# A mixture-of-experts kernel whose sort by expert becomes lists in DRAM, filled chunk by chunk during conditioning

## The chip, the cores and the metric

One core of one Trainium2 chip. The metric is the device time of one execution in microseconds.

## What is computed

```python
def cond(x, W, A, Bm, scalings, adapter_idx):      # x: 64 x 64 x 512, f32
    delta = (x @ A[adapter_idx].T) @ Bm[adapter_idx].T * scalings[adapter_idx]
    return x @ W.T + delta                         # rank 16, 8 adapters
def ffn(x, ...):                                   # 4096 tokens of 512
    shared = sum(gelu(x @ Wsh_up[e]) @ Wsh_down[e] for e in range(2))
    top_v, top_i = top_k(softmax(x @ W_router), 2) # of 16 experts
    routed = sum(top_v[r] * gelu(x @ Wrt_up[top_i[r]]) @ Wrt_down[top_i[r]] for r in range(2))
    return shared + routed                         # hidden 256 per expert
out = x + ffn(cond(x))
```

## The kernel before, in words

4096 tokens are 16 chunks of 256 (`NC`), each two tiles of 128. Most fp32 products are done as three fp16 products: each matrix is scaled by a power of two taken from its largest magnitude, a high half is rounded to fp16 (ScalarE) and the low half is what is left (VectorE or GpSimd). Every engine runs its own written-out queue; semaphores order them.

**Conditioning.** For each chunk c TensorE's `cond_step` (L1278) does the adapter input (L1238), two tiles of x @ W (L1249) with the transposes of chunk c-1 (L1265) between, the router logits of c-1 (L1274) and the adapter output (L1257). VectorE's step is `search_step` (L971) for chunks up to 7 and `low_step` (L1026) from chunk 8: `mask_xa` (L875, the first of a step), `row_max`, `x_low` for chunk c+1, `x_largest` for chunk c+2 (L947), maxima of arriving expert weights (`lot_maxima`, L906) or the low halves of two experts (`low_routed`, L935), `x_scales` (L952) and `top` (L881: logits copied, the two best of 16 and their indices, L883 to L893). GpSimd spreads the maximum of x over the partitions by an all-reduce (`x_reduce`, L521). Chunks 0 and 1 are multiplied whole in fp32 (`whole=True`), from chunk 2 on in halves. SyncE's `cond_chunk` (L352) loads chunk c+3, stores rows and transposes of chunk c, and `weights_chunk` issues the next two expert loads, each after a wait on `lot_max_ready`; the load of the next x stands behind these.

**Sort.** After the last chunk VectorE makes one-hots of all tokens (L1051), TensorE their prefix sums (L1301), VectorE a scan over 32 tiles (L1063, L1064), the start of each expert's tiles (L1067 to L1081), the place of each token (L1083 to L1093) and the scales of the whole conditioned x, whose maximum comes back by way of DRAM (L404, L914). Then `places` (L1101) compares iotas with each place (L1107, L1108), 64 times two instructions, and `inversion_products` (L1310, matmul L1313) turn them on TensorE into `tok`, the token of each slot. `sorted_ready` lets GpSimd gather rows (`gather`, L566).

**Early shared passes.** Meanwhile TensorE does the shared experts of chunks 0 to 5 (`EARLY`): `shared_up` (L1327, 48 matmuls) and `shared_down` (L1340, 24), in an order written out by hand with the sort's products between. ScalarE rounds the high halves (L662, L767) and writes a scaled copy (L664, L769), from which GpSimd subtracts (`low_condT` L542, `low_hid` L547); GpSimd also does `add_x` (L537).

**Routed tiles.** 79 tiles of 128 slots, pipelined: transpose (L1377), up (L1393), transpose of the middle (L1402), down (L1412). GpSimd gathers the rows (L574).

**Late stage.** The shared passes of chunks 6 to 15, while GpSimd gathers routed rows back (L608) and VectorE adds them weighted (L1168).

What sets the order: an engine's instructions start in the order written, so what stands behind a wait waits as well. This is all that decides it on SyncE's and GpSimd's queues of DMAs too.

```python
with pe.Fori(1, A_HALF) as i:
    cond_step(2 * i, i, 0)
    cond_step(2 * i + 1, i, 1)
```

## Time and profile before

| what | us |
|---|---|
| median of 3 runs | 679.23 (679.11 to 682.99) |
| the profiled execution | 681.92 |
| its span, first to last instruction | 679.9 |
| mean granted TensorE clock | 0.974 |

The profile is one execution, so the sums are made against 681.92. Times in a timeline count from the start of the span. PE is TensorE, PEld its weight load, DVE VectorE, ACT ScalarE, POOL GpSimd, SP SyncE. "[3.63 <-DMA ...]" is the idle time of that engine just before the instruction and what ended it. The granted clock is in shares of full speed, 2.4 GHz. L is a line of the kernel.

### The profile page before, as it was taken

To read this page: it belongs to the slowest core of one execution; us is meant where nothing else is said; L and a number is where in the kernel's file an instruction comes from. 1 tells how busy PE (TensorE), PEld (TensorE's weight loads), DVE (VectorE), ACT (ScalarE), POOL (GpSimd) and SP (SyncE) were. 2 spreads that over 40 slices of the span, in tenths; PEclk is the share of its full clock that TensorE was granted. 3 is DMA by queue.
4 is the path that set the end of the run, shared out by engine and by line. 5 is a ranking of instruction groups with operands and counts; after the bars stand their busy time and mean duration, and the time that the engine had idled before them with its cause. 6 is when DMAs were issued, how large, how long until landed. Compare 5 with 4: busy or idle time off the path is not lost.

```text
span 679.9 us, 13742 instructions
## 1 busy us (share of the span) xinstructions
PE 627.5 (92%) x4115; PEld 428.4 (63%) x4117; DVE 457.4 (67%) x900; ACT 327.2 (48%) x480; POOL 222.6 (33%) x288
## 2 busy tenths in 40 slices
PE   4998999999989758889999999999999999989794
PEld 2465656566657435556777777777777777665561
DVE  2779999999974998525555555555555554688674
ACT  1333224677775743464555555555555554333230
POOL 1000000101012742373333333333333306777771
PEclk9997999999998988999999999999999999999898
DMA  7688994343334312165555555555555539989966
GB/s 275 281 312 286 374 346 168 123 157 142 132 127 128 124 63 93 32 217 171 159 159 169 161 154 159 164 168 157 156 159 167 164 107 377 366 301 362 369 205 248
DMA packets 49765, 135.68 MB, mean 200 GB/s; under 512 B 6160, under 2 KB 6288, under 8 KB 47312
## 3 DMA queue, kind: packets, MB, share of 16 engines
q1 hardware_dynamic: 38304, 97.93, 39.1%
q0 software_dynamic: 11440, 37.50, 20.0%
q8 instruction: 11, 0.18, 0.1%
q14 instruction: 10, 0.08, 0.0%
HBM read 86.38 MB, written 49.02 MB: 199 GB/s over the span
## 4 chain that ended last, share of the span: by engine, by line
PE 53%; DVE 17%; POOL 12%; issue 7%; DMA 7%; ACT 1%; SPq 0%; DVEq 0%; POOLq 0%; ACTq 0%
PE bank L1412 15%; PE bank L1393 14%; POOL rtw L608 9%; PE bank L1249 7%; PE bank L1377 5%; DVE lot_max L906 5%; DMA act_in<-xT 3%; PE bank L1402 2%; PE bank L1327 2%; PE bank L1257 2%; PE bank L1274 2%; DMA region<-xc_dram,slot_idx 2%; PE bank L1238 1%; DVE x_max L947 1%; PE bank L1265 1%
## 5 line engine op out<-in xcount | busy, mean ns | idle before, releaser
L1129 DVE SCALAR_TENSOR_TENSOR region<-bank,scale,region 128x512 f16<-128x512 f32 x79 | 59.2, 751 | 128.7 <-ACT region L809 128.7
L1393 PE MATMUL bank<-rtw,region 128*128 x948 | 116.4, 273 | 0.0
L1412 PE MATMUL bank<-rtw,tmp 128*128 x474 | 115.2, 379 | 0.6 <-DVE tmp L1137 0.6
L1393 PEld LDWEIGHTS bank<-rtw,region 128*128 128x128 f16 x948 | 92.8, 98 | 10.1
L1340 PE MATMUL bank<-shw,hid 128*128 128x512 f16 x384 | 91.3, 397 | 8.3 <-DVE rtw L1193 7.7
L574 POOL DMA_INDIRECT region<-xc_dram,slot_idx x79 | 77.1, 976 | 61.3 <-POOL slot_idx L571 61.3
L1327 PE MATMUL bank<-act_in,shw 128*128 128x256 f16 x768 | 89.4, 277 | 2.9 <-ACT tmp L756 1.7
L1327 PEld LDWEIGHTS bank<-act_in,shw 128*128 128x128 f16 x768 | 75.8, 100 | 16.0 <-ACT tmp L756 2.2
L816 ACT ACTIVATE region<-bank,un_dn 128x512 f32<-128x512 f32 x79 | 54.3, 687 | 57.3 <-PE bank L1412 54.8
L608 POOL DMA_INDIRECT rtw<-r_dram,row_idx x64 | 70.0, 1093 | 27.6 <-issue 14.8
L1340 PEld LDWEIGHTS bank<-shw,hid 128*128 128x128 f16 x384 | 38.4, 102 | 56.4 <-issue 10.0
L1412 PEld LDWEIGHTS bank<-rtw,tmp 128*128 128x128 f16 x474 | 46.3, 98 | 39.2 <-issue 1.3
L805 ACT ACTIVATE tmp<-bank,un_up 128x256 f32<-128x256 f32 x79 | 37.4, 473 | 60.2 <-PE bank L1393 60.2
L1168 DVE SCALAR_TENSOR_TENSOR rtw<-rtw,gate 128x512 f32 (+1 forms) x64 | 45.4, 750 | 15.2 <-DMA rtw<-r_dram,row_idx 13.0
L809 ACT ACTIVATE region<-bank,scale 128x512 f16<-128x512 f32 x79 | 54.1, 687 | 2.2 <-PE bank L1377 2.2
L523 POOL PARTITION_ALL_REDUCE x_max_all<-x_max x14 | 10.7, 763 | 134.9 <-DVE x_max L949 134.9
L1377 PE MATMUL bank<-ident,region 128*128 128x128 f32 x316 | 47.4, 273 | 2.6 <-DMA region<-xc_dram,slot_idx 2.5
L571 POOL COPY slot_idx<-tok 128x1 int32 (+1 forms) x79 | 14.4, 182 | 106.5 <-PE bank L1377 97.0
L756 ACT ACTIVATE tmp<-bank,un_up 128x256 f32<-128x256 f32 x44 | 20.4, 471 | 52.2 <-PE bank L1327 49.9
L641 ACT ACTIVATE rtw<-rtw,scale 128x1024 f16<-128x1024 f32 (+1 forms) x32 | 35.8, 1152 | 17.3 <-DVE rtw L935 15.1
L935 DVE SCALAR_TENSOR_TENSOR rtw<-rtw,scale 128x1024 f16<-128x1024 f32 x32 | 39.6, 1279 | 4.4 <-ACT rtw L641 4.3
L1135 DVE TENSOR_SCALAR tmp<-bank,to_mid 128x256 f16<-128x256 f32 x79 | 38.2, 484 | 6.1 <-PE bank L1402 2.7
(157 smaller groups left out, 910.0 us busy)
## 6 DMA issues: line engine op xcount, KB each, us to landing
r_dram<-region SPq DMA_DIRECT2D x79, 256.0 KB
rtw<-rt_w SPq DMA_DIRECT2D x16, 1024.0 KB, 7.4
act_in<-xT SPq DMA_DIRECT2D x16, 512.0 KB, 3.8
xc_dram<-rows SPq DMA_DIRECT2D x16, 512.0 KB, 3.7
xcT_dram<-hid SPq DMA_DIRECT2D x16, 512.0 KB, 2.8
rtw<-x_rows SPq DMA_DIRECT2D x16, 512.0 KB, 5.4
rtw<-xcT_dram SPq DMA_DIRECT2D x13, 512.0 KB, 6.1
out<-rtw SPq DMA_DIRECT2D x9, 512.0 KB, 5.6
```

The lines of the kernel that those rows point to most:

```text
L574: nc.gpsimd.indirect_dma_start(out=xg[s], out_offset=None, in_=xc_dram, in_offset=bass.IndirectOffsetOnAxis(ap=slot_idx[s][:].bitcast(U32) ...
L608: nc.gpsimd.indirect_dma_start(out=routed_row(slot, r, t), out_offset=None, in_=r_dram, in_offset=bass.IndirectOffsetOnAxis(ap=row_idx[slo ...
L809: nc.scalar.activation(xgT[s][:, 0], R_XT[s][:].rearrange("p (k t) -> p k t", k=HK), ACT.Copy, scale=col(scale, C_ALL).bitcast(F32)).then_ ...
L816: nc.scalar.activation(rrow[s], R_DN[s][:], ACT.Copy, scale=col(un_dn, ROUTED)).then_inc(rrow_ready, 1)
L1129: nc.vector.scalar_tensor_tensor(xgT[s][:, 1], R_XT[s][:].rearrange("p (k t) -> p k t", k=HK), col(scale, C_ALL).bitcast(F32), xgT[s][:, 0 ...
L1168: last = nc.vector.scalar_tensor_tensor(y, routed_row(slot, r, t), gate[:, r, bass.ds(c * NT + t, 1)], y, ALU.mult, ALU.add)
L1249: last = mm(COND[NT * s + t][:], act_in[s][:, k, at] if whole else xp[s][:, ap, k, at], w_in[:, k, :] if whole else wt[:, bp, k, :], start ...
L1327: last = mm(UP[em % 2][:, 0:CHUNK], shw[:, e, w0:w0 + P], actT[s][:, xp, k, :], start=(k == 0 and n == 0), stop=(k == HK - 1 and n == 2))
L1340: last = mm(DOWN[t][:], hidT[s][:, xp, em, t * P:(t + 1) * P], shw[:, em // DM, w0:w0 + H], start=(em == 0 and n == 0), stop=(em == EM - 1 ...
L1377: last = nc.tensor.transpose(R_XT[s][:, k * P:(k + 1) * P], xg[s][:, k * P:(k + 1) * P], ident[:])
L1393: last = mm(R_UP[s][:, 0:D], xgT[s][:, xp, k, :], rtw[:, bass.ds(e, 1), w0:w0 + D].rearrange("p a d -> p (a d)"), start=(k == 0 and n == 0 ...
L1412: last = mm(R_DN[s][:], midT[s][:, xp, m, :], rtw[:, bass.ds(e, 1), w0:w0 + H].rearrange("p a h -> p (a h)"), start=(m == 0 and n == 0), s ...
```

## The change

- **Lists.** A DRAM tensor `lists` has 4096 places for each expert. After `top` VectorE makes the chunk's one-hot; GpSimd's `count` adds them up and keeps the running count over earlier tiles; TensorE's `rank_products`, in the same turn as a later router product, give every token's rank; VectorE's `list_places` turns expert and rank into a place two steps later; GpSimd's `scatter` writes 128 token numbers by an indirect DMA, four a chunk. At the end VectorE works out from which 128-entry list each tile comes, GpSimd gathers these and TensorE transposes them into `tok`. The slot of each token for the way back (`pos`) is worked out after that.
- **Maxima.** The maximum per partition is put on a diagonal, TensorE multiplies it by ones (`spread_x`, `spread`) and VectorE reduces the row. The all-reduces and the way through DRAM are gone.
- **Chunk 1** is multiplied in halves; only chunk 0 whole. Its x comes into the place of expert 12's weights. The small loads are issued first and chunk 2's x before the shared weights.
- **Low halves** of the early shared passes are made by VectorE straight from the unscaled source; ScalarE's scaled copies are gone, GpSimd keeps `add_x`.
- `x_scales` stands after both `low_routed`, and the load of chunk 2's transpose is issued earlier.

The diff, cut to its core:

```diff
--- before
+++ after
+        lists = nc.dram_tensor("lists", [E_RT * LIST, P], F32, kind="Internal").ap()
...
-            sp.dma_start(at_in, AT).then_inc(w_adapters, 16)
-            sp.dma_start(flat(act_in[0][:]), chunk_T(xT, 0)).then_inc(act_loaded[0], 16)
             sp.dma_start(sc_col[:], scal).then_inc(w_mask, 16)
             sp.dma_start(idx_b[:], idx.partition_broadcast(P)).then_inc(w_mask, 16)
+            sp.dma_start(at_in, AT).then_inc(w_adapters, 16)
+            sp.dma_start(flat(x_first), chunk_T(xT, 0)).then_inc(first_loaded, 16)
             for dst, src in ((w_in, WT), (bmt, BmT), (wr, w_r)):
                 sp.dma_start(dst, src).then_inc(w_cond, 16)
-            sp.dma_start(flat(act_in[1][:]), chunk_T(xT, 1)).then_inc(act_loaded[1], 16)
+            for c in range(1, 3):
+                sp.dma_start(flat(act_in[c % 2][:]), chunk_T(xT, c)).then_inc(act_loaded[c % 2], 16)
+            sp.wait_ge(masks, 5)
+            sp.dma_start(lists.rearrange("(p a) n -> p (a n)", p=P), lg[:].rearrange("p t e -> p (t e)")).then_inc(lists_cleared, 16)
             sp.dma_start(arrived(0), sh_up).then_inc(w_shared, 16)
             sp.dma_start(spare, sh_dn).then_inc(w_shared, 16)
-            sp.wait_ge(act_used, 1)
-            sp.dma_start(flat(act_in[0][:]), chunk_T(xT, 2)).then_inc(act_loaded[0], 16)
...
+            sp.wait_ge(condT_half, 1)
+            load_condT(2, 0, early_condT(2))
...
-            def x_reduce(c, s):
-                pool.wait_ge(x_max_ready, c - 1)
-                nc.gpsimd.partition_all_reduce(x_max_all[s][:], x_max[s][:], P, RMAX).then_inc(x_reduced, 1)
...
+            def count(k, s):
+                at = slice(NT * k, NT * k + NT)
+                pool.wait_ge(top_ready, k + 1)
+                if k > 1:
+                    pool.wait_ge(rank_read, k - 1)
+                if k:
+                    nc.gpsimd.tensor_tensor(earlier[s][:, 0, :], earlier[1 - s][:, 1, :], oh_sum[1 - s][:, 1, :],
+                                            ALU.add)
+                nc.gpsimd.tensor_copy(best[:, at, :], best_c[s][:, :, 0:K_TOP])
+                nc.gpsimd.tensor_copy(chosen[:, :, at], best_i_c[s][:, :, 0:K_TOP].rearrange("p t r -> p r t"))
+                nc.gpsimd.tensor_tensor(oh_sum[s][:], oh[s][:, 0], oh[s][:, 1], ALU.add).then_inc(summed, 1)
+                pool.wait_ge(summed, k + 1)
+                nc.gpsimd.tensor_tensor(earlier[s][:, 1, :], earlier[s][:, 0, :], oh_sum[s][:, 0, :], ALU.add).then_inc(counted, 1)
+                pool.wait_ge(counted, k + 1)
+            def scatter(k):
+                pool.wait_ge(slot_ready, k + 1)
+                for r in range(K_TOP):
+                    for n in range(NT * k, NT * k + NT):
+                        nc.gpsimd.indirect_dma_start(
+                            out=lists.rearrange("a (n o) -> (a n) o", o=1),
+                            out_offset=bass.IndirectOffsetOnAxis(ap=pos[:, r, n:n + 1].bitcast(U32), axis=0),
+                            in_=tok_no[:, n:n + 1], in_offset=None,
+                        ).then_inc(scattered, 16)
+            pool.wait_ge(lists_cleared, 16)
+            for c in range(1, NC):
+                if c > 2:
+                    scatter(c - 3)
+                count(c - 1, (c - 1) % 2)
+            scatter(NC - 3)
+            count(NC - 1, 1)
+            scatter(NC - 2)
+            scatter(NC - 1)
+            pool.wait_ge(list_ready, 1)
+            pool.wait_ge(scattered, 16 * K_TOP * TT)
+            nc.gpsimd.indirect_dma_start(
+                out=tokT, out_offset=None, in_=lists,
+                in_offset=bass.IndirectOffsetOnAxis(ap=list_i[:].bitcast(U32), axis=0),
+            ).then_inc(tokT_loaded, 16)
...
-            low_condT(0)
-            low_condT(1)
-            for c in range(EARLY - 2):
-                low_hid(c)
-                low_condT(c + 2)
-                if c:
-                    add_x((c - 1) // 2, (c - 1) % 2)
-            low_hid(EARLY - 2)
+            for c in range(2):
+                add_x(0, c)
...
-                last = nc.scalar.activation(actT[s][:, 0], by_block(src), ACT.Copy, scale=by)
-                if early:
-                    last = nc.scalar.activation(src, src, ACT.Copy, scale=by)
-                last.then_inc(condT_half, 1)
+                nc.scalar.activation(actT[s][:, 0], by_block(src), ACT.Copy, scale=by).then_inc(condT_half, 1)
...
             def top(c, s):
+                at = slice(c * NT, c * NT + NT)
                 dve.wait_ge(logit_ready, c + 1)
+                nc.vector.tensor_copy(lg[:, at, :], LOGIT[:, 0:NT * E_RT].rearrange("p (t e) -> p t e", t=NT)).then_inc(logit_copied, 1)
                 dve.wait_ge(logit_copied, c + 1)
-                nc.vector.tensor_copy(lg[:, bass.ds(c * NT, NT), :], lg_c[s][:])
                 for t in range(NT):
+                    nc.vector.max(best_c[s][:, t, :], lg[:, c * NT + t, :]).then_inc(best_ready, 1)
                 dve.wait_ge(best_ready, c * NT + NT)
-                nc.vector.tensor_copy(best[:, bass.ds(c * NT, NT), :], best_c[s][:, :, 0:K_TOP])
                 for t in range(NT):
                    ...
                 dve.wait_ge(place_found, c * NT + NT)
-                nc.vector.tensor_copy(chosen[:, :, bass.ds(c * NT, NT)],
-                                      best_i_c[s][:, :, 0:K_TOP].rearrange("p t r -> p r t")).then_inc(top_ready, 1)
+                nc.vector.tensor_tensor(oh[s][:], iota_e[:].unsqueeze(1).unsqueeze(1).to_broadcast([P, K_TOP, NT, E_RT]),
+                                        best_i_c[s][:, :, 0:K_TOP].rearrange("p t r -> p r t").unsqueeze(3).to_broadcast([P, K_TOP, NT, E_RT]),
+                                        ALU.is_equal).then_inc(top_ready, 1)
+            def list_places(k, s):
+                at = slice(k * NT, k * NT + NT)
+                if k + 1 < NC:
+                    dve.wait_ge(logit_ready, k + 2)
+                else:
+                    dve.wait_ge(ranked, 1)
+                nc.vector.tensor_tensor(placed[:], oh[s][:], PLACE.unsqueeze(1).to_broadcast([P, K_TOP, NT, E_RT]),
+                                        ALU.mult).then_inc(rank_read, 1)
+                dve.wait_ge(rank_read, k + 1)
+                nc.vector.tensor_reduce(rank[:, :, at], placed[:], AX_X, ALU.add).then_inc(rank_found, 1)
+                dve.wait_ge(rank_found, k + 1)
+                nc.vector.scalar_tensor_tensor(pos[:, :, at], chosen[:, :, at], float(TOK), rank[:, :, at],
+                                               ALU.mult, ALU.add).then_inc(slot_ready, 1)
...
+                dve.wait_ge(x_max_ready, c)
+                nc.vector.tensor_scalar(x_diag, ident[:], x_max[s][:], None, ALU.mult).then_inc(x_diag_ready, 1)
             def x_scales(c, s):
-                dve.wait_ge(x_reduced, c - 1)
+                if c < 3:
+                    dve.wait_ge(spread_ready, c)
+                else:
+                    dve.wait_ge(logit_ready, c - 2)
+                nc.vector.tensor_reduce(x_max_all[s][:], SPREAD[:, 2, :], AX_X, ALU.max).then_inc(x_all_found, 1)
+                dve.wait_ge(x_all_found, c)
...
+            x_largest(1, 1)
+            spread_out(LIN_W, SH_UP)
+            find_all(LIN_W, SH_UP)
             scales(1, LIN_W, SH_UP)
...
+            x_scales(1, 1)
+            x_largest(2, 0)
...
             low_linear(at_[:, 1], at_in, LIN_A, at_[:, 0], 2)
-            dve.wait_ge(scale_ready, 1)
...
+            low_x(1, 1)
+            x_scales(2, 0)
+            mask_xa(1, 1)
+            row_max(0, 0)
+            low_x(2, 0)
+            dve.wait_ge(w_shared, 2 * 16)
...
+            top(0, 0)
+            lot_maxima((0, 1))
             search_step(1, 0, [(0, 2), (0, 3), (1, 0)])
...
                 low_routed(2 * c - NC)
+                low_routed(2 * c - NC + 1)
+                if c == NC - 1:
+                    low_condT(0, 0, early_condT(0), C_EARLY)
                 if more:
                     x_scales(c + 2, s)
-                low_routed(2 * c - NC + 1)
                 top(c - 1, 1 - s)
+                list_places(c - 2, s)
...
+            early_low_condT(1)
+            early_low_hid(0)
+            find_all(C_ALL, C_ALL + 1)
             top(NC - 1, 1)
-            dve.wait_ge(top_ready, NC)
-            for r in range(K_TOP):
-                link(nc.vector.tensor_tensor(oh[r][:], iota_e[:].unsqueeze(1).to_broadcast([P, TT, E_RT]),
-                                             chosen[:, r, :].unsqueeze(2).to_broadcast([P, TT, E_RT]), ALU.is_equal))
-            nc.vector.tensor_tensor(oh_sum[:], oh[0][:], oh[1][:], ALU.add).then_inc(onehot_ready, 1)
-            link(nc.vector.tensor_tensor(lg[:], lg[:], best[:, :, 0:1].to_broadcast([P, TT, E_RT]), ALU.subtract))
-            nc.vector.tensor_tensor(best[:, :, 1:2], best[:, :, 1:2], best[:, :, 0:1], ALU.subtract).then_inc(shifted_ready, 1)
-            dve.wait_ge(prefix_ready, 1)
-            link(nc.vector.tensor_copy(acc0, TOT[:].rearrange("p (t e) -> p t e", t=TT)))
...
-            link(nc.vector.tensor_scalar(cnt_i[:], src[:, TT - 1, :], float(P - 1), None, ALU.add))
+            list_places(NC - 2, 0)
+            early_low_condT(2)
+            scales(4, C_ALL, C_ALL + 1)
+            result_scales(SH_REST, C_ALL, SH_UP, SH_DN)
+            result_scales(ROUTED, C_ALL, RT_UP, RT_DN)
+            early_low_hid(1)
+            list_places(NC - 1, 1)
...
+            early_low_condT(3)
+            early_low_hid(2)
             dve.wait_ge(tile_row_ready, 1)
             for n in (0, 2):
...
+            dve.wait_ge(inverted, 1)
+            nc.vector.tensor_copy(tok[:], INV[:, 0:NJ_ALL]).then_inc(sorted_ready, 1)
+            early_low_condT(4)
+            early_low_hid(3)
...
-            def places(i, first=False):
...
+            dve.wait_ge(scattered, 16 * K_TOP * TT)
+            for r in range(K_TOP):
+                link(nc.vector.tensor_tensor(acc, iota_e[:].unsqueeze(1).to_broadcast([P, TT, E_RT]),
...
+                link(nc.vector.tensor_reduce(starts[:, r, :], acc, AX_X, ALU.add))
+            nc.vector.tensor_tensor(pos[:], starts[:], rank[:], ALU.add).then_inc(pos_ready, 1)
+            early_low_condT(5)
+            early_low_hid(4)
...
+            def spread_x(c):
+                pe.wait_ge(x_diag_ready, c)
+                return mm(SPREAD[:, 2, :], ones[:], x_diag, start=True, stop=True)
+            def rank_products(k, s):
+                pe.wait_ge(counted, k + 1)
+                mm(PLACE, lower[:], oh_sum[s][:], start=True, stop=False)
+                return mm(PLACE, ones[:], earlier[s][:], start=False, stop=True)
...
+            def cond_step(c, i, s, more=True, middle=False, second=False):
...
+                router_products(c - 1, 1 - s, peaks_of=c + 2 if more else None, ranks_of=c - 2, second=second)
...
+            def token_transpose():
+                pe.wait_ge(tokT_loaded, 16)
+                nc.tensor.transpose(INV[:, 0:P], tokT, ident[:]).then_inc(inverted, 1)
...
-            router_products(NC - 1, 1)
+            pe.wait_ge(logit_copied, NC - 1)
+            spread(4, 1)
+            router_products(NC - 1, 1, ranks_of=NC - 2)
             shared_up(0, 1)
-            prefix_products()
+            last_rank_products()
             shared_down(0, 0, first=True)
             shared_up(1, 0)
             tile_expert_product()
             shared_down(0, 1)
+            token_transpose()
             shared_up(1, 1)
-            inversion_products(0)
             shared_down(1, 0)
-            inversion_products(1)
-            inversion_products(2)
             shared_up(2, 0)
-            inversion_products(3)
-            inversion_products(4)
             shared_down(1, 1)
-            inversion_products(5)
-            inversion_products(6)
-            shared_up(2, 1, blocks=range(2))
-            inversion_products(7)
-            shared_up(2, 1, blocks=range(2, EM))
+            shared_up(2, 1)
             shared_down(2, 0)
```

## Rows read from the trace of the kernel before

**Rows 1.** The page of the profile: the chain that ended last, by engine
```profile
PE 53%; DVE 17%; POOL 12%; issue 7%; DMA 7%; ACT 1%; SPq 0%; DVEq 0%; POOLq 0%; ACTq 0%
```

**Rows 2.** Stretches: stretch, length, busy per engine (instructions), PE clock, DMA share, GB/s
```profile
150.00:200.00 50.00, 48.81 (x285) 31.06 (x283) 44.97 (x96) 35.65 (x41) 3.93 (x3) 1.00 0.34 126
...
240.00:260.00 20.00, 12.61 (x78) 7.67 (x77) 19.03 (x67) 7.47 (x10) 6.55 (x3) 0.74 0.15 54
...
320.00:560.00 240.00, 240.00 (x1764) 179.48 (x1763) 126.39 (x221) 132.84 (x220) 79.52 (x138) 1.00 0.54 157
```

**Rows 3.** Timeline of VectorE, conditioning: start, busy us, engine, line, operation, idle before
```profile
12.31 2.29 DVE L994 TENSOR_REDUCE largest<-rtw 128x1 f32<-128x2048 f32 x1 [2.02 <-DMA region<-w_r]
...
42.71 0.42 DVE L875 TENSOR_TENSOR xam<-bank,mask 128x256 f32<-128x256 f32 x1
...
49.15 1.22 DVE L947 TENSOR_REDUCE x_max<-act_in 128x1 f32<-128x1024 f32 x1 [3.63 <-DMA act_in<-xT]
...
62.71 1.22 DVE L947 TENSOR_REDUCE x_max<-act_in 128x1 f32<-128x1024 f32 x1 [1.38 <-DMA act_in<-xT]
...
117.96 0.42 DVE L875 TENSOR_TENSOR xam<-bank,mask 128x256 f32<-128x256 f32 x1
...
128.18 0.17 DVE L893 CAST chosen<-best_i_c 128x4 f32<-128x4 uint32 x1
128.26 0.42 DVE L875 TENSOR_TENSOR xam<-bank,mask 128x256 f32<-128x256 f32 x1
```

**Rows 4.** Timeline of TensorE: the first products of chunks 14 and 15
```profile
176.91 1.47 PE L1238 MATMUL bank<-tmp,region 128*128 128x256 f16 x12
...
187.78 1.47 PE L1238 MATMUL bank<-arena,region 128*128 128x256 f16 x12
```

**Rows 5.** Timeline of TensorE, shared passes, sort and first tiles
```profile
202.63 6.25 PE L1327 MATMUL bank<-act_in,shw 128*128 128x256 f16 x48
...
253.60 0.71 PE L1313 MATMUL bank<-region 128*128 128x80 f16 x8 [7.39 <-DVE region L1108]
...
262.28 5.41 PE L1327 MATMUL bank<-act_in,shw 128*128 128x256 f16 x48
...
270.86 5.35 PE L1340 MATMUL bank<-shw,hid 128*128 128x512 f16 x24
...
296.30 1.47 PE L1393 MATMUL bank<-rtw,region 128*128 x12
...
318.58 1.47 PE L1393 MATMUL bank<-rtw,region 128*128 x12
```

**Rows 6.** Timeline of VectorE, sort: small operations
```profile
244.66 0.20 DVE L1092 CAST arena<-arena 128x64 f32<-128x64 int32 x1
...
245.12 0.28 DVE L914 TENSOR_REDUCE largest_all<-xam 128x1 f32<-128x128 f32 x1
...
246.72 0.25 DVE L1107 TENSOR_SCALAR region<-iota_p,arena 128x128 f16<-128x128 f16 x1
```

**Rows 7.** Timeline of GpSimd: a low half, and an indirect DMA of the last stage
```profile
200.36 2.13 POOL L542 TENSOR_TENSOR act_in<-tmp,act_in 128x1024 f16<-128x1024 f32 x1 [25.34 <-ACT tmp L664]
...
564.13 0.95 POOL L608 DMA_INDIRECT rtw<-r_dram,row_idx  x1 [0.30 <-issue]
```

**Rows 8.** Grouped lines of 200 to 296 us: busy us, mean ns, idle before
```profile
L1108 DVE TENSOR_SCALAR region<-iota_j,arena,tok_no 128x80 f16<-128x80 f16 x64 | 22.4, 349 | 0.0
...
L542 POOL TENSOR_TENSOR act_in<-rtw,act_in 128x1024 f16<-128x1024 f32 x4 | 8.5, 2124 | 6.4 <-ACT rtw L664 6.4
...
L769 ACT ACTIVATE tmp<-tmp,to_mid 128x1024 f32<-128x1024 f32 x6 | 6.8, 1133 | 0.0
```

**Rows 9.** The chain in order of time: a gather of the first tiles, from issue to landing
```profile
300.26 4.62 DMA region<-xc_dram,slot_idx
```

**Rows 10.** Timeline of VectorE: a cast at the end of conditioning
```profile
200.51 2.00 DVE L893 CAST chosen<-best_i_c 128x4 f32<-128x4 uint32 x1
```

**Rows 11.** The page, costliest groups: the weighing of the last stage
```profile
L1168 DVE SCALAR_TENSOR_TENSOR rtw<-rtw,gate 128x512 f32 (+1 forms) x64 | 45.4, 750 | 15.2 <-DMA rtw<-r_dram,row_idx 13.0
```

More of the change, by code:

```diff
@@ L682, in cond_rows @@
                     act.wait_ge(cond_ready, NT * c + t + 1)
-                    if first:
+                    if whole:
                         ins = nc.scalar.copy(rows[s][:, t, :], COND[NT * s + t][:])
@@ L1294, in _ @@
             pe.wait_ge(lin_split, 2)
[L1295 to L1304 removed]
+            adapter_inputs(1, 0, 1)
@@ new lines, in _ @@
+            cond_products(1, 1, 0, first=True)
+            cond_transposes(0, 0, first=True)
+            cond_products(1, 1, 1, first=True)
+            pe.wait_ge(x_all_found, 2)
+            spread(2, 2)
+            router_products(0, 0, peaks_of=3, first=True)
+            adapter_products(1, 1)
+            pe.wait_ge(all_found, 2)
+            cond_step(2, 1, 0, second=True)
+            cond_step(3, 1, 1)
+            with pe.Fori(2, A_HALF // 2) as i:
+                for s in range(2):
+                    cond_step(2 * i + s, i, s)
```

392 lines of the change are left out of this document (193 added, 199 removed).

## The prediction

> **What bounds the kernel now.** I read the page first, then the busy time by stretches, then the timelines of VectorE, TensorE and GpSimd, last the grouped lines of the sorting stage. The chain that ended last is only 53% TensorE and 17% VectorE [rows 1]: there are stages with another limit. The stretches tell them apart [rows 2]. From 150 to 200 us TensorE is busy 48.81 of 50 us and VectorE 44.97; from 240 to 260 us TensorE does 12.61 of 20 us at a granted clock of 0.74 while VectorE does 19.03; from 320 to 560 us TensorE does 240.00 of 240. So:
> - Conditioning, up to about 127 us: VectorE's own queue. Its step 2 begins at 42.71 and step 8 at 117.96; it waits for x at 49.15 and at 62.71 [rows 3], and from there on for nothing.
> - Conditioning after that: TensorE, 10.87 us a chunk (176.91 to 187.78) [rows 4], while a VectorE step takes 10.30 (117.96 to 128.26) [rows 3]. That gap of 0.57 us is all the room there is.
> - Shared passes and sort, 202.63 to 296.30 [rows 5]: 93.7 us. VectorE's sort holds TensorE up (7.39 us idle for L1108 at 253.60), and what TensorE then does is slow.
> - Routed tiles: a tile has 12+6+4+2 = 24 matmul records, 1764/24 = 73.5 tiles in 240 us, 3.27 us each [rows 2]. Nothing in it is changed, nor in the last stage but a wait on `pos_ready` that was met long before.
>
> **The change: conditioning.** Per step VectorE loses three small copies in `top` (each lets the next begin some 0.08 later: L893 at 128.18, L875 at 128.26 [rows 3]): -0.25. It gains the one-hot compare of 128x64 (0.20 as L1092 [rows 6], less overlap: 0.13); `list_places`, three instructions that wait for each other (0.20, 0.20, 0.15 and the gaps: 0.60); the diagonal of 128x128 (0.25 as L1107, with its wait 0.33); the reduction of 128x128 out of PSUM (0.28 as L914, and the gap behind it: 0.32). Sum +1.13 us a step. From below it is 0.6, if more of it overlaps; from above 1.6, if GpSimd's small operations get in the way.
> - Start. Two tables are found before x can be split, and chunk 1 in halves needs the split weights. In the new order, with the old durations, VectorE reduces W and A from 12.31 [rows 3] to 15.2, does `x_largest(1)` 1.6, diagonals 0.7, `find_all` 0.5 and `scales` 0.6 (`scale_ready` at 18.9), then `x_scales(1)`, `x_largest(2)`, the mask and W's low halves to 24.7, x's to 26.0, where the halves of chunk 1 may start; chunk 2's by 30.2, the two shared maxima by 34.7, `x_largest(3)` and a lot by 39.0, scales, `top(0)` and the second lot by 44.0. So step 2 begins at about 44.0 and not 42.71: +1.3. TensorE's saving of some 2 us on chunk 1 is hidden: VectorE is later.
> - Steps 2 to 7: 6 x 1.13 = +6.8, and +0.7 for the three maxima before step 8, which now make a turn through TensorE. Before, VectorE waited 3.63 and 1.38 us for x [rows 3]. SyncE issues that load only after the `lot_max` waits ahead of it, so the first wait moves along and the second is filled: -1.8. Step 8 begins at 117.96 + 1.3 + 6.8 + 0.7 - 1.8 = 125.0, **+7.0**.
> - Steps 8 to 13: a VectorE step is now 10.30 + 1.13 = 11.43. A TensorE step gets three small products; eight of 128x80 took 0.71 [rows 5], so at most +0.27: 11.05 to 11.14. VectorE becomes the bound. TensorE's step 14 needs `x_diag` of step 13 (4.3 us into VectorE's step), then 3.7 us of router and adapter: it starts at 125.0 + 5 x 11.43 + 8.0, and step 15 at +11.05: 201.2, against 187.78. That is +13.5 in all, so **+6.5** here.
> - GpSimd gets four scatters a chunk, 1.25 us apart (0.95 + 0.30 [rows 7]), and five small operations: some 7 us of 11.4. It doesn't bound, and the counts that `rank_products` waits for are two chunks old. What is queued behind that wait on TensorE is the router, for which VectorE waits.
> - At the end the second ScalarE copy of chunk 0 goes (L769's like: 1.13 us a piece [rows 8]): **-1.0**. The first shared pass begins at 202.63 + 12.5 = 215.1.
>
> **The change: shared passes.** All 64 x 2 compares of the inversion go (L1108 alone 22.4 us [rows 8]), the scan over 32 tiles and the round trip of the maximum through DRAM. VectorE gets the low halves, 12 of about 1.2 us (the size of its row at L947 [rows 3]), in place of GpSimd's of 2.12 [rows 8]. TensorE at full pace: six up passes of 5.3 (5.41 busy) and six down passes of 5.2 [rows 5] = 63.0, last router 1.8, transposes and small products 1.6: 66.4. I add 1.1 for the first Gelus and 1.5 for the token list, which is the tightest turn. Counted from the start of the first pass: last ranks 13; `list_places(15)`, behind a low half, 16.4; its scatters, behind those of chunk 14, until 23.3; landed 26; gather issued 26.8, landed 29 to 31; TensorE is at `token_transpose` at 29.2. The landing is a choice: a row gather took 4.62 from issue [rows 9] with 4 times the bytes (128 rows of 2 KB, not of 512 B). So 69.0 instead of 93.7: **-24.7**. The 0.74 of clock [rows 2] stood in a stretch in which TensorE sat idle; the passes at 5.41 and 5.35 us stood in one with the clock at 1.00, and I take those.
>
> **First tiles.** GpSimd did low halves between the gathers. Up products 0 and 6 lie 22.3 us apart (296.30, 318.58 [rows 5]); at the pace it would be 2.3 and 3.3 for the first two and 4 x 3.26: 18.6, so 3.7 were lost. Now only `add_x` is between: **-3.0**.
>
> GpSimd's long operations also held VectorE: a cast of 128x4, elsewhere 0.17 [rows 3], took 2.00 at 200.51 [rows 10] beside L542 of 200.36 to 202.49 [rows 7]. Ten of these go, and with them stalls that my 69.0 already leaves out.
>
> *By the Trainium skill (SBUF — State Buffer, Who interferes with whom)* a copy, cast or tensor-scalar of VectorE in a two-port mode and a GpSimd instruction exclude each other for the whole instruction. The 2.00 us row agrees. The page counts descriptor writing as GpSimd's use of the port; that speaks against scatters in a stage bound by VectorE, and is the third rival.
>
> **Sum.** 7.0 + 6.5 - 1.0 - 24.7 - 3.0 = -15.2 us. The profiled execution took 681.92 (span 679.9 and 2.0 around it), so 666.7; the median is 2.7 lower: **664 us**.
>
> **Rivals.**
> 1. VectorE's additions are hidden. For: the 0.57 us of room, and the waits for x. Against: VectorE waits for nothing from 64 to 127 us [rows 3]. If they cost 0.6 a step, stage two stays TensorE's (8 x 0.2 = 1.6 for 6.5) and stage one loses 3 us less: 656.
> 2. The token list is late. Each us by which it misses 29.2 is a us of TensorE, and `low_condT(4)` and `low_hid(3)` are queued behind the wait on VectorE (needed only at 40). If scatter and gather each take 4.62 to land [rows 9], 9.2 instead of the 5.9 above: +3.3; if `list_places(15)` slips by one high and one low half, +2.3: 670.
> 3. Scatters hold VectorE up, so slower than before. For: the cast of 2.00 us [rows 7, 10]. Against: in the last stage L1168 with two SBUF inputs keeps 750 ns [rows 11] beside 64 gathers of the same form; but it is no copy or tensor-scalar, so the row doesn't exclude it. Place: steps 2 to 15, 56 scatters. It decides from (679.2 - 664)/56 = 0.27 us of VectorE per scatter. If every second one costs a whole 0.95 [rows 7]: +27, 691. The page's rule would give just this.
>
> **Chances.** Forecast 0.60 (own range 659 to 671), rival 1 0.14, rival 2 0.16, rival 3 0.10. A measurement here tells about 1% (6.8 us) from no change: faster means under 672.4. Of the forecast 0.56 is below it, all of rival 1, of rival 2 0.11: faster 0.81. Same: 0.04 + 0.05 + 0.01 = 0.10. Slower: 0.09, all of it rival 3. Range: from 652 (rival 1 with a gain of 4 us more in the passes, where I set 2.6 for stalls) to 678 (rival 2 with the upper price of a step, 0.47 x 12 = 5.6 us on top, and 2 us for x loads behind the small writes of the lists, of which no row has the like).
>
> **What would show it.** Right: VectorE's steps 11.4 us apart from step 8 to 13 and TensorE waiting for `x_diag` or `xam` there; the first shared pass at 213 to 217; then TensorE without idle time over 2 us up to the first routed product, at full clock, 69 us later; a wait, if any, at `token_transpose`. Wrong: steps of 10.9 (rival 1), a wait of over 3 us at `token_transpose` (rival 2), VectorE copies or tensor-scalars of about 1 us beside scatters (rival 3), or a first shared pass after 225.

## The result, and the profile after

The changed kernel takes 716.04 us (median of 4 executions, 710.1 to 720.74) where the kernel before took 679.49 beside it: ratio 1.0521, 95% interval 1.0435 to 1.0608. Forecast were 664 and a gain. The profiled execution took 720.74 us, its span is 719.0.

From the page of the changed kernel: the chain that ended last, by engine; the two busiest DMA queues (packets, MB, share of the 16 DMA engines); and two of the DMA issue rows (count, KB each, us from issue to landing).

```profile
PE 50%; DMA 16%; DVE 13%; POOL 9%; issue 7%; ACT 2%; SPq 1%; POOLq 0%; ACTq 0%; DVEq 0%
...
q1 hardware_dynamic: 38160, 98.12, 45.4%
q0 software_dynamic: 13520, 37.60, 19.1%
...
rtw<-rt_w SPq DMA_DIRECT2D x16, 1024.0 KB, 15.2
...
act_in<-xT SPq DMA_DIRECT2D x15, 512.0 KB, 8.5
```

VectorE's share of the chain fell from 17% to 13%, and DMA now holds 16%, where it was 7% [rows 1]. That is no work of an engine that computes: it is waiting for transfers. The stretches say when (columns as in [rows 2]):

```profile
60.00:100.00 40.00, 24.00 (x133) 15.70 (x132) 23.61 (x50) 8.50 (x11) 10.69 (x18) 0.76 0.96 180
100.00:150.00 50.00, 37.12 (x182) 22.01 (x182) 31.47 (x70) 10.45 (x15) 20.66 (x27) 0.84 0.94 198
150.00:200.00 50.00, 44.54 (x234) 27.88 (x235) 42.21 (x96) 24.57 (x29) 15.44 (x27) 0.82 0.51 108
```

The kernel before, from 60 to 100 us:

```profile
60.00:100.00 40.00, 38.57 (x209) 23.96 (x210) 38.11 (x70) 12.05 (x17) 1.05 (x3) 0.94 0.96 355
```

Read the last two columns together. The 16 DMA engines are as busy as before (0.96), and move half as much: 180 GB/s where it was 355. TensorE and VectorE both do 24 us of work in 40. The queues of that window, before, then after (packets, MB, share of the 16 engines), say where the busy time goes:

```profile
q1 hardware_dynamic: 3315, 14.21, 96.1%
...
q1 hardware_dynamic: 1668, 7.19, 94.4%
q0 software_dynamic: 256, 0.00, 1.0%
```

The packets of the scatters (q0, GpSimd's queue) take 1.0% of the engines' time. It is the packets of all other transfers (q1, SyncE's queue) that take about twice as long each as before. The waits of conditioning (20 to 230 us; engine, tile and line, releaser: us in total, times, longest):

```profile
DVE x_max L980 <- DMA act_in<-xT: 38.4, 4, 15.3
PE bank L1315 <- DVE tile_e L985: 40.3, 7, 16.0
```

TensorE waits for VectorE's diagonal, and VectorE for x. Its timeline, the first instruction of some steps and the waits for x:

```profile
44.18 0.41 DVE L878 TENSOR_TENSOR xam<-bank,mask 128x256 f32<-128x256 f32 x1
51.90 1.22 DVE L980 TENSOR_REDUCE x_max<-act_in 128x1 f32<-128x1024 f32 x1 [4.92 <-DMA act_in<-xT]
63.02 0.42 DVE L878 TENSOR_TENSOR xam<-bank,mask 128x256 f32<-128x256 f32 x1 [0.52 <-PE bank L1283]
76.25 0.42 DVE L878 TENSOR_TENSOR xam<-bank,mask 128x256 f32<-128x256 f32 x1
94.31 1.22 DVE L980 TENSOR_REDUCE x_max<-act_in 128x1 f32<-128x1024 f32 x1 [15.25 <-DMA act_in<-xT]
...
127.05 1.22 DVE L980 TENSOR_REDUCE x_max<-act_in 128x1 f32<-128x1024 f32 x1 [5.93 <-DMA act_in<-xT]
...
153.28 1.22 DVE L980 TENSOR_REDUCE x_max<-act_in 128x1 f32<-128x1024 f32 x1 [12.32 <-DMA act_in<-xT]
...
166.58 0.41 DVE L878 TENSOR_TENSOR xam<-bank,mask 128x256 f32<-128x256 f32 x1
```

Step 2 begins at 44.18 (forecast 44.0) and step 3 at 63.02. The first scatter is issued at 63.6 (the row of L536 below); from then on the waits are long, and step 8 begins at 166.58 where 125.0 was forecast and 117.96 measured before [rows 3]. What changed in the transfers, window 60 to 100 us, median us from issue to landing; of before, then of after:

```profile
rtw<-rt_w SPq DMA_DIRECT2D x7, 1024.0 KB, 7.4
act_in<-xT SPq DMA_DIRECT2D x4, 512.0 KB, 6.5
xc_dram<-rows SPq DMA_DIRECT2D x3, 512.0 KB, 8.3
```

```profile
rtw<-rt_w SPq DMA_DIRECT2D x4, 1024.0 KB, 19.4
xc_dram<-rows SPq DMA_DIRECT2D x2, 512.0 KB, 15.0
act_in<-xT SPq DMA_DIRECT2D x2, 512.0 KB, 24.8
lists<-tok_no,pos POOLq DMA_INDIRECT x8, 11.5
```

The other transfers take about two to four times as long, and a scatter of 128 words (512 B in all) takes 11.5 us to land. Later, TensorE's shared passes:

```profile
259.97 5.51 PE L1420 MATMUL bank<-act_in,shw 128*128 128x256 f16 x48
...
288.83 5.30 PE L1420 MATMUL bank<-act_in,shw 128*128 128x256 f16 x24 [7.58 <-ACT tmp L762]
...
299.56 0.27 PE L1408 MATMUL bank<-ident,arena 128*128 128x128 f32 x1
...
337.20 1.47 PE L1478 MATMUL bank<-rtw,region 128*128 x12
```

The first pass begins 57.3 us later than before (202.63 [rows 5]), and from it to the first routed product pass 77.2 us: less than the 93.7 before, more than the forecast's 69.0. The 7.58 us go back to a transfer as well: ScalarE waited 5.64 us for the load of a chunk's transpose, which stood behind a store that landed 18.5 us after its issue.

### The profile page after: what moved, and what is told of

Same layout as the page of the kernel before. It is cut to its first block, busy times and chain, and to the rows that moved or that the text cites. A ratio compares the mean times of both kernels' runs of the same rounds, so it can differ in the third digit from the quotient of the medians.

```text
span 719.0 us, 13717 instructions
## 1 busy us (share of the span) xinstructions
PE 640.1 (89%) x4120; PEld 434.8 (60%) x4121; DVE 442.2 (62%) x835; ACT 316.0 (44%) x468; POOL 274.1 (38%) x402
## 4 chain that ended last, share of the span: by engine, by line
PE 50%; DMA 16%; DVE 13%; POOL 9%; issue 7%; ACT 2%; SPq 1%; POOLq 0%; ACTq 0%; DVEq 0%
PE bank L1497 14%; PE bank L1478 14%; DMA act_in<-xT 9%; POOL rtw L614 8%; PE bank L1462 5%; PE bank L1294 3%; PE bank L1302 3%; PE bank L1341 3%; DMA xcT_dram<-hid 3%; DVE rtw L968 3%; PE bank L1487 2%; PE bank L1283 2%; PE bank L1420 2%; DVE x_max L980 2%; DMA rtw<-xcT_dram 2%
## 5 line engine op out<-in xcount | busy, mean ns | idle before, releaser
L1433 PE MATMUL bank<-shw,hid 128*128 128x512 f16 x384 | 88.7, 389 | 8.4 <-DVE rtw L1238 8.4
L536 POOL DMA_INDIRECT lists<-tok_no,pos x64 | 71.6, 1119 | 25.8 <-issue 14.6
L808 ACT ACTIVATE tmp<-bank,un_up 128x256 f32<-128x256 f32 x79 | 37.4, 473 | 60.9 <-PE bank L1478 60.9
L690 ACT ACTIVATE rows<-bank,un_cond 128x512 f32<-128x512 f32 x30 | 20.2, 683 | 91.8 <-PE bank L1302 91.6
L522 POOL TENSOR_TENSOR earlier<-earlier,oh_sum 128x16 bf16<-128x16 bf16 x15 | 3.2, 212 | 128.6 <-DVE oh L895 128.6
L1294 PE MATMUL bank<-region,arena 128*128 128x512 f16 x192 | 44.0, 379 | 0.0
## 6 DMA issues: line engine op xcount, KB each, us to landing
rtw<-rt_w SPq DMA_DIRECT2D x16, 1024.0 KB, 15.2
```

Source lines behind the costliest of these rows:

```text
L536: nc.gpsimd.indirect_dma_start(out=lists.rearrange("a (n o) -> (a n) o", o=1), out_offset=bass.IndirectOffsetOnAxis(ap=pos[:, r, n:n + 1]. ...
L1294: last = mm(COND[NT * s + t][:], x_first[:, k, at] if whole else xp[s][:, ap, k, at], w_in[:, k, :] if whole else wt[:, bp, k, :], start=( ...
L1433: last = mm(DOWN[t][:], hidT[s][:, xp, em, t * P:(t + 1) * P], shw[:, em // DM, w0:w0 + H], start=(em == 0 and n == 0), stop=(em == EM - 1 ...
```

## Experiments

Two theories to begin with: A, the scatters' writes keep the DMA engines from the other transfers; B, something else of the change makes x late. In e1, e2, e3, e7, e8, g2 and h3 the lists that are read hold a ramp, so the amount of work behind the sort stays and the tokens in the slots are others. Beside them the kernel before took 684.33 us (e1 to e4) and 688.36 (e5 to e8), one execution each, and medians of 680.0 (g1 to g4) and 680.7 (h1 to h3); in these two sets its executions lie between 677.3 and 687.1. The changed kernel, g1, h1 and h3 are medians of 4 to 10 executions; the other times are single executions, so differences of under some 10 us between them say nothing.

**e1: no scatter.**

```diff
-                        nc.gpsimd.indirect_dma_start(out=lists..., in_=tok_no[:, n:n + 1], ...).then_inc(scattered, 16)
-            pool.wait_ge(scattered, 16 * K_TOP * TT)
```

> The changed kernel without its 64 scatters: counts, ranks and places are worked out as before, but nothing is written into the lists, which hold made-up token numbers from the start, so the routed rows are other ones (the output is not the reference's). Theory A (the 4-byte writes slow every other transfer, and VectorE then waits for x): the waits of VectorE for x, 38 us in the changed kernel, fall to some 4 us, the first shared pass begins at 214 to 217 us and the whole takes 662 to 670 us, which is the forecast. Theory B (VectorE's longer step and the new order of SyncE's issues alone make the loads late): the waits for x stay above 25 us and the whole above 700.

670.48 us, 45.6 less than the changed kernel's median. From 60 to 100 us:

```profile
60.00:100.00 40.00, 39.07 (x207) 22.98 (x206) 38.06 (x86) 13.11 (x19) 4.75 (x15) 0.88 0.81 298
```

TensorE and VectorE work again, and 298 GB/s come out of a smaller DMA share, 0.81. One wait for x is left (4.6 us). A holds and B falls: 64 instructions that write 32 KB in all cost some 46 us. The numbers written for A are missed by a little (670.48 for at most 670, the first shared pass at 220.52 for 214 to 217): a part of the miss is not the scatters'.

**e4: the kernel before, with 44 scatters** of made-up indices (16 targets 16 KB apart, the words of each target within 32 B), four a chunk in steps 5 to 15, nothing else changed.

```diff
+                if c > 4:
+                    for n in range(4 * (c - 5), 4 * (c - 5) + 4):
+                        nc.gpsimd.indirect_dma_start(out=lists, out_offset=...fake[:, n:n + 1]..., in_=tok_no[...])
```

> The kernel of before, to which nothing is added but 44 scatters of 128 words of 4 bytes into a table that nobody reads, four after each of GpSimd's all-reduces of chunks 5 to 15. VectorE's steps stay as they were. Theory A: VectorE gets waits for x of 20 us or more in all between 60 and 150 us, and the whole takes 700 us or more. Theory B: within 5 us of 680, since GpSimd has room for the issues.

718.88 us, 34.6 more than its neighbour, with 26.8 us of waits for x between 60 and 150 us, as theory A has it. The same picture in a kernel that is otherwise untouched:

```profile
60.00:100.00 40.00, 33.88 (x156) 21.18 (x156) 30.34 (x54) 8.96 (x13) 11.09 (x13) 0.76 1.03 228
```

From 20 to 230 us:

```profile
DVE x_max L963 <- DMA act_in<-xT: 40.8, 10, 14.5
```

(A DMA share above 1 can't be literal; read it as full.) The scatters alone do it. What of them: that the writes are small, that they are many, or where they go?

**e2: the same words, each on a row of its own**, 512 B apart, in a tensor of its own. **e3: 128 rows of 512 B** to the same places, 128 times the bytes.

```diff
+        wide = nc.dram_tensor("wide", [E_RT * TOK, P], F32, kind="Internal").ap()
-                            out=lists.rearrange("a (n o) -> (a n) o", o=1),
+                            out=wide.rearrange("a (n o) -> (a n) o", o=1),   # e2, with pos times 128
+                            out=wide, in_=ident[:],                          # e3
```

> The changed kernel, with its 4-byte writes put 512 bytes apart in a table of 32 MB, so that no two of them fall into one line of memory; one small VectorE operation more a chunk (0.2 us each); made-up token numbers in the lists (the output is not the reference's). If neighbouring words collide (theory A3): waits for x below 15 us, the whole 665 to 685. If smallness alone counts (A1): as slow as the changed kernel, 700 to 725.

> The changed kernel, where each scatter writes 128 rows of 512 bytes (64 KB) to places 512 bytes apart in a table of 32 MB, instead of 128 words; the lists hold made-up token numbers (the output is not the reference's). Theory A1 (it is the smallness of the writes): though 128 times the bytes are written, 4 MB more in all, which at the 355 GB/s of the loaded stage are 12 us of the DMA engines, the waits for x fall below 20 us and the whole is 665 to 690. Theory A2 (any scatter, whatever its rows): 716 or more.

e2 took 675.3 and e3 674.96, with waits for x of 3.7 and 4.5 us. So neither the size of a write nor their number costs much: as many writes of 4 B to other places are nearly free, and so are writes of 512 B. So it must be the place.

**e7 and e8: words 32 B and 64 B apart**, the rest as in e2.

```diff
-                nc.vector.scalar_tensor_tensor(pos..., float(TOK), rank...).then_inc(slot_ready, 1)
+                link(nc.vector.scalar_tensor_tensor(pos..., float(TOK), rank...))
+                nc.vector.tensor_scalar(pos[:, :, at], pos[:, :, at], float(8), None, ALU.mult).then_inc(slot_ready, 1)  # e8: 16
```

> As the kernel whose words lie 512 bytes apart, but 32 bytes apart (a table of 2 MB). If what collides is a piece of memory of 32 bytes or less: 670 to 680 as with 512 bytes. If it is 64 bytes (two words to a piece instead of sixteen): waits for x of 5 to 25 us, the whole 680 to 705. If smallness of the table or nearness of the experts' lists counts, not the piece: 710 or more.

> The same with words 64 bytes apart (a table of 4 MB). If the piece is 32 or 64 bytes: 670 to 680. If it is larger (256 or 512 bytes): 685 to 710, between the kernel with 4 bytes and that with 512.

679.3 and 674.03, waits for x of 3.8 and 4.8 us. Not being next to each other is enough, down to 32 B.

**e6: words adjacent as in the change, but each expert's list 16.5 KB after the last one instead of 16 KB.**

```diff
-        lists = nc.dram_tensor("lists", [E_RT * LIST, P], F32, kind="Internal").ap()
+        lists = nc.dram_tensor("lists", [E_RT * (LIST + 1), P], F32, kind="Internal").ap()
-                nc.vector.scalar_tensor_tensor(pos[:, :, at], chosen[:, :, at], float(TOK), rank[:, :, at],
+                nc.vector.scalar_tensor_tensor(pos[:, :, at], chosen[:, :, at], float(TOK + P), rank[:, :, at],
```

> The changed kernel with the words next to each other as they were, but each expert's list 4224 words long instead of 4096, so that the sixteen places at which a scatter writes are no longer 16 KB apart. If neighbouring words collide (A3): no help, 705 to 725. If the sixteen lists fall into one bank of memory because of the power of two (theory A4): 665 to 685.

679.48 beside 688.36, waits for x 4.9 us, first shared pass at 224.69. The words lie as close to each other as in the changed kernel, and the cost is gone. So adjacency isn't the cause by itself, nor is the pitch (e2, e7 and e8 have pitches of 2 MB, 128 KB and 256 KB, powers of two as well). What the bad layouts share is both: all 128 writes of a scatter fall into one short stretch modulo 16 KB, since the 16 lists grow at about the same pace from starts 16 KB apart.

**e5: scatters only from step 8 on**, eight a step, when the weights are through.

```diff
-                if c > 2:
-                    scatter(c - 3)
...
+                if c >= 8:
+                    for k in (2 * (c - 8), 2 * (c - 8) + 1) if c < 13 else (c - 3,):
+                        scatter(k)
```

> The changed kernel, word for word, but the scatters wait: none before step 8 of conditioning, then eight a step until they have caught up at step 13. Up to step 8 no scatter can hold a load up: waits for x before 125 us fall to some 5 us and step 8 begins at 125 instead of 166. After that the loads of x have 8 us of slack. If the harm is bound to the stage in which the DMA engines are full: 675 to 685. If it goes with the number of scatters wherever they stand: x is late from step 9 on, 700 or more.

734.68. Up to step 8, which begins at 129.12, nothing is disturbed: x waits of 4.0 us. The first scatter is issued at 141.9, and then the stage from 150 to 200 us, in which the kernel before has a DMA share of 0.34 and 126 GB/s [rows 2], looks like this:

```profile
150.00:200.00 50.00, 24.55 (x120) 14.98 (x119) 19.21 (x51) 12.79 (x15) 19.21 (x28) 0.70 1.06 48
```

Only 11.1 us of the loss show as a wait for x. The rest is not followed here; ScalarE, for one, stands idle for 25.8 us before its copies into `hid` (L700), with no releaser that the profile names. The first shared pass begins at 260.35. The harm follows the scatters to wherever they stand; it isn't the contest with the weights' loads, and it needs no stage in which the DMA engines are nearly full.

**g1: e6 timed; g2, g3, g4: how far apart the lists have to be** (adjacent words).

```diff
-                ...chosen[:, :, at], float(TOK), rank[:, :, at], ...
+                ...chosen[:, :, at], float(TOK + 8), rank[:, :, at], ...      # g2: 16 KB + 32 B
+                ...chosen[:, :, at], float(TOK + 8 * P), rank[:, :, at], ...  # g3: 20 KB
+                ...chosen[:, :, at], float(2 * TOK), rank[:, :, at], ...      # g4: 32 KB
```

> The kernel of e6_pitch again (each expert's list 4224 words after the last, 16.5 KB, not 4096), now timed in rounds against the kernel before. Theory A4 (a scatter's 128 words all fall into a few places modulo 16 KB): the cure holds, x waits under 5 us, first shared pass at 221 to 226, ratio to the kernel before 0.975 to 0.99, so 663 to 673 where that takes 679 to 680. Rival (the single look at 679.48 beside 688.36 was chance, and what is left of the scatters' cost is still about 10 us): ratio 0.99 or more.

> Adjacent words, each expert's list 4104 words after the last: 16 KB and 32 B, in a tensor of its own; the lists that are gathered hold a ramp, so the slots' tokens are wrong. Theory A4a (what counts is how many places of a few tens of bytes the 128 writes fall into, modulo 16 KB; 16 experts now cover 16 x 32 = 512 B): cured, x waits under 6 us, first shared pass at 221 to 228, 670 to 682. Theory A4b (a place is as wide as 512 B or more): no cure, an x wait of about 15 us, first shared pass after 250, 705 or more.

> Adjacent words, each expert's list 5120 words after the last: 20 KB, so the 16 lists lie 4 KB apart modulo 16 KB and fall into 4 places instead of 16. Theory A4 with a period of 16 KB: four times as many places as in the changed kernel, so the harm of 46 us falls to a quarter or to nothing: 670 to 690, first shared pass at 221 to 235. Theory A4c (the period is 4 KB or less): all 16 lists in one place as in the changed kernel, 705 or more, first shared pass after 250.

> Adjacent words, each expert's list 8192 words after the last: 32 KB. Theory A4 with a period of 16 KB (or of 32 KB): nothing changes, 705 or more, an x wait of 12 to 15 us, first shared pass after 250. Theory with a longer period: two or more places, 670 to 695, first shared pass before 240.

| kernel | lists apart | starts modulo 16 KB | us | waits for x, us | GB/s, 60:100 |
|---|---|---|---|---|---|
| changed | 16 KB | all one | 716.04 | 38.4 | 180 |
| g2 | 16 KB + 32 B | 32 B steps, 512 B in all | 715.26 | 33.2 | 190 |
| g4 | 32 KB | all one | 701.31 | 24.6 | 230 |
| g3 | 20 KB | four, 4 KB apart | 690.69 | 15.2 | 274 |
| g1 | 16.5 KB | 16, 512 B apart | 676.18 | 6.5 | 276 |

g1 is 0.9926 of the kernel before (0.9889 to 0.9963). That is outside the 0.975 to 0.99 written for theory A4, and in the rival's 0.99 or more: the cure holds, but what was written for it was too good. g2 decides for a place at least a few hundred bytes wide. g3 lands just above what was expected of four places (690.69 for 670 to 690, the first shared pass at 235.77 for 221 to 235). g4 fits neither of its two expectations: with a period of 16 KB it should have been as bad as the changed kernel, and it isn't, by 14.7 us (8.8 under the fastest execution of the changed kernel); for a longer period it is too slow. So "modulo 16 KB" is a summary of the direction, not the map: a wider spread costs less, and the period stays open. e7 is the second loose end. Its lists start a multiple of 16 KB apart as well, and its words, some eight a list and 32 B apart, cover 256 B, less than the 512 B of g2's starts, which cure nothing; yet e7 is undisturbed. By this picture it could be so only if the lists differ in length by tens of entries, since each entry of difference moves e7's words by 32 B and g2's by 4. No run measured that.

**h1: lists 17 KB apart. h2: the kernel before with e4's scatters, targets 16.5 KB apart. h3: e1 timed.**

```diff
+                ...chosen[:, :, at], float(TOK + 2 * P), rank[:, :, at], ...  # h1
+            link(nc.vector.tensor_scalar(extra[:], raw_i[:], (E_RT - 1) * TOK, None, ALU.bitwise_and))  # h2
+            link(nc.vector.tensor_scalar(extra[:], extra[:], 1.0 / 32.0, None, ALU.mult))
+            link(nc.vector.tensor_tensor(raw_i[:], raw_i[:], extra[:], ALU.add))
```

> The changed kernel with each expert's list 4352 words (17 KB) after the last: the 16 lists lie 1 KB apart modulo 16 KB and so over the whole of it, where the pitch of 16.5 KB covers half. Theory A5 (the wider the words of a scatter are spread modulo 16 KB, the less it costs): ratio to the kernel before 0.985 to 0.992, 1 to 5 us under the pitch of 16.5 KB. Rival (16.5 KB already takes away all that the pitch can): ratio 0.990 to 0.996, as that one's 0.9926.

> The kernel before with the 44 made-up scatters of e4_before_scatter, but the 16 targets 4224 words (16.5 KB) apart and not 4096. Theory A4 (the places decide, whatever the kernel): 680 to 692 where e4_before_scatter took 718.88, and no wait for x over 6 us. Rival (in the changed kernel it was an accident of its timing, or of its indices): 705 or more.

> The kernel of e1_no_scatter again (no scatter, lists cleared with a ramp, so tokens not those of the sort), timed in rounds. If the forecast without the scatters' cost on the DMA engines is right (664 for 679.2): ratio 0.978. With e1's single look (670.48, where its neighbour before took 684.33): 0.980. So 0.975 to 0.985 says that spread scatters still cost 5 to 12 us; 0.99 or more says that they cost nothing and that the forecast's own sum is 8 us short.

- h1: 676.86, ratio 0.9947 (0.9912 to 0.9982). Not to be told from g1; a wider spread brings no more, so theory A5 (0.985 to 0.992) falls.
- h2: 681.68 beside 680.7, where e4 took 718.88. In the stretch from 60 to 100 us, against e4's row above:

```profile
60.00:100.00 40.00, 38.44 (x209) 23.53 (x208) 37.97 (x70) 12.04 (x17) 13.19 (x16) 0.94 1.02 321
```

- h3: 672.34, ratio 0.9882 (0.9845 to 0.992). So spread scatters still cost some 4 us: h1, beside it, takes 676.86, and nine of its ten executions are above the slowest of h3's four (673.12), though the intervals of the two ratios overlap a little. The change without any is 8 us faster than before and not 15. Its ratio stands a little over the 0.975 to 0.985 that was written for it, under the 0.99 of the other branch: both have a part.

## Why the prediction was wrong

The step that failed is one phrase of the range, "2 us for x loads behind the small writes of the lists, of which no row has the like", and the sentence "GpSimd gets four scatters a chunk [...] It doesn't bound". I priced a scatter on the engine that issues it, and GpSimd indeed doesn't bound. But what its 128 writes do to the other transfers stands in the sum at nothing, and in the range at 2 us for all 64. They cost some 44 (716.04 against h3's 672.34; 45.6 by e1's one execution). The bound was set without a row near it, and there was none: the gathers move rows of 2 KB [rows 9].

h3 shows how the rest of the sum stood, since it differs from the changed kernel in the scatters, the waits for them and the tokens in the slots alone:

| step of the forecast | before | forecast | no scatters (h3) | changed kernel |
|---|---|---|---|---|
| VectorE's step 2 begins | 42.71 | 44.0 | 45.1 | 44.2 |
| step 8 begins | 117.96 | 125.0 | 130.4 | 166.6 |
| a step, mean of 8 to 13 | 10.31 | 11.43 | 11.81 | 11.86 |
| first shared pass | 202.63 | 215.1 | 221.8 | 260.0 |
| from there to the first routed product | 93.7 | 69.0 | 65.9 | 77.2 |
| first to seventh up product | 22.3 | 19.3 | 20.6 | 20.5 |
| span | 679.9 | 664.7 | 670.0 | 719.0 |

- **Steps 2 to 7.** The price per step was near. From step 2 to step 8 the forecast has 81.0 us with 3.2 of waiting, so 77.8 of work; h3 has 85.3 with 6.8, so 78.5, 0.1 a step more. The one-hot takes 0.23 us, `list_places` 0.21, 0.22 and 0.17, the diagonal 0.29, the reduction 0.28. "The first wait moves along and the second is filled: -1.8" was half right: h3 has 0.49 us for x left in step 3, where the kernel before had 1.38, but 4.26 in step 2 for 3.63, and a wait for TensorE before step 7 that the sum had not:

```profile
52.18 1.22 DVE L973 TENSOR_REDUCE x_max<-act_in 128x1 f32<-128x1024 f32 x1 [4.26 <-DMA act_in<-xT]
...
116.33 0.42 DVE L871 TENSOR_TENSOR xam<-bank,mask 128x256 f32<-128x256 f32 x1 [2.07 <-PE bank L1275]
```

  So 3.6 us more of waiting (6.8 for 3.63 + 1.38 - 1.8), a start 1.1 later and 0.7 of work make the 5.4 by which step 8 is late.
- **Steps 8 to 13.** "VectorE becomes the bound" is right: undisturbed steps of h3 take 11.55 (141.95 to 153.50), and TensorE waits for the diagonal (0.27 at 146.53). One of the five takes 12.42 (165.27 to 177.69), with 0.8 us of waiting for ScalarE's high halves (L961 for L640), which the sum had not. +1.9 over five steps.
- **Shared passes.** Right: h3, in which no list has to land, takes 65.9; g1, in which the lists work as meant, takes 68.4 (221.59 to 289.98) for the forecast's 69.0. Its `token_transpose` stands at 251.06, 29.5 after the first pass (forecast 29.2), behind 0.56 us of waiting for the gathered lists. So the list is the tight turn that the forecast saw, and rival 2, a list late by 3 us and more, didn't happen. (In the changed kernel, at 299.56, there is no wait, but TensorE is late there itself.)
- **First tiles.** 1.7 us won and not 3.0; the second tile still waits 1.18 us for its gather.
- Added up for h3: +19.2 - 27.7 - 1.7 = -10.2, and its span is 9.9 under before's. The forecast had +12.5 - 24.7 - 3.0.
- **Slips in the working.** Step 15 at 201.2 is 13.4 later than before, not 13.5. VectorE does wait once between 64 and 127 us (0.50 us for GpSimd at 116.45). The scatters of steps 2 to 15 are 52, not 56: the first is issued in step 3. None of these moves the forecast by more than 0.1 us.
- **Rival 3, the scatters hold VectorE up by the shared port**, gave the right sign and 691 us, by a mechanism that is there and is worth half a microsecond. Of the changed kernel (min, median and max ns):

```profile
L887 DVE COPY lg<-bank x16: 178/180/191, 40.9 to 270.0; 128x32 f32<-128x32 f32 x16
...
L985 DVE TENSOR_SCALAR tile_e<-ident,x_max x15: 286/286/288, 16.1 to 230.1; 128x128 bf16<-128x128 f32 x15
...
L998 DVE TENSOR_SCALAR x_scale<-x_expo x15: 143/144/145, 19.0 to 235.9; 128x1 int32<-128x1 int32 x15
...
L536 POOL DMA_INDIRECT lists<-tok_no,pos x64: 954/984/1897, 63.6 to 286.5; - x64
```

  Between 60 and 290 us 34 copies, casts and tensor-scalars of VectorE overlap a scatter's instruction on GpSimd. Three of them are long, and each ends within 0.02 us of the scatter's end. The second of them:

```profile
262.34 1.00 POOL L536 DMA_INDIRECT lists<-tok_no,pos  x1 [0.47 <-POOL earlier L528]
...
262.96 0.40 DVE L933 TENSOR_SCALAR tile_e<-ident,peaks 128x128 bf16<-128x128 f32 x1
```

  It takes 0.40 us for 0.29 in h3. The others are L952 at 165.83 (0.31 for 0.17) and L1150 at 285.71 (0.42 for 0.17). That is 0.5 us in all, where the rival needed 27. The rule cited there from the Trainium skill (SBUF — State Buffer, Who interferes with whom) is borne out by these three; the other 31 are within 0.03 us of their usual length, which the prediction's "if every second one costs a whole 0.95" did not allow for. Some scatters are long too (up to 1.90 us for 0.98); what holds them up is not shown.

The chances were at fault beside the size: none of the three rivals was about what a new kind of transfer does to the transfers beside it. The forecast didn't look at the DMA engines at all, whose share from 60 to 100 us was 0.96 already. That share alone would not have given the answer either: e5 shows more harm in a stage where it was 0.34.

## What to carry to other kernels

Price a new transfer three times: on the engine that issues it, on the DMA engines (how late may the other transfers of that stage come?), and by where its writes fall. A scatter into lists that start a power of two apart and grow in step aims all its writes at nearly the same places; half a kilobyte of padding per list was worth 40 us here. And when DMA engines are as busy as before but move half the bytes, look for small writes on another queue and for where they fall, not for a lack of bandwidth.

Of the versions whose lists hold the right tokens the padded one (g1) takes least, 676.18 against 680.0: 0.7% (interval 0.4 to 1.1%), a gain that is there and is under the 1% that the prediction counted as a change.

## What the runs showed of the hardware

- 128 words written by one indirect DMA took 11.5 us to land and halved the rate of all other transfers (355 to 180 GB/s at a DMA share of 0.96), with 16 lists 16 KB apart. With lists 16.5 KB apart (g1) the scatters landed in 6.9 us in the same window and the rate was 276. The scatters' own packets took 1.0% of the engines' time in the slow case.
- The Trainium skill (DMA: Bandwidth & Descriptors, Latency and other measured facts) has a neighbour of this: copies of large tiles slow down where the rows of a tensor stand 2 MB to 8 MB apart, padding a pitch of 4 MB by 4 KB cures it and by 192 B doesn't; it calls a shared memory channel an inference. The runs here agree in kind at a far smaller pitch and with writes of one word: 32 B of padding did nothing (715.26), 512 B was enough (676.18). Whether it is the same mechanism no run here shows.
- The Trainium skill (DMA: Bandwidth & Descriptors, Specifications) states that transfers under 512 B make the engine read, change and write back. Taken alone it would have every scatter of single words cost alike; in these runs the kernel with 4-byte writes 64 B apart took 674.03 us, the one with adjacent ones 716.04.
- Beside a scatter's instruction on GpSimd three of 34 copies, casts and tensor-scalars of VectorE were longer by 0.12 to 0.25 us and ended with it; the others were not.
- Left open: the period and the width of a "place" (g4 against g3, e7 against g2), and whether the packets are held up in the memory or on the way to it. No run looks behind the DMA engines.
